# Where the second sample's half slots stand in a fused four-layer block: token layer from half slot 2, offsets projected ahead, mask summed a slot later, convolution's adds three half slots further back

## The reference, cut to what matters

```python
def reference(x, ...):                      # x: 16 x 128 x 56 x 56, f32
    x = x + _L0_conv_ref(_gn(x), ...)       # whitening of 8 channel groups
    x = x + _L1_conv_ref(_gn(x), ...)       # deformable convolution: depthwise 3x3, norm, GELU,
                                            #   offsets and mask by a matmul, mask softmax,
                                            #   bilinear samples weighted by the mask, out matmul
    x = x + _L2_conv_ref(_gn(x), ...)       # attention in 7x7 windows, a token per window,
                                            #   attention over the tokens, aggregate, out matmul
    x = x + _L3_conv_ref(_gn(x), ...)       # mask from the centre of mass, relu, 3x3 convolution
    return x
```

## Time and profile before

| | us |
|---|---|
| median of 3 runs | 11108.46 |
| lowest and highest run | 11075.77, 11125.28 |
| the profiled execution, its own time | 11137.82 |
| its span | 11135.9 |
| PE busy | 8908.2 (80% of the span) |
| DVE busy | 7395.0 (66%) |
| ACT busy | 3642.6 (33%) |
| mean granted TensorE clock | 0.848 of full speed |

### The profile page before, as it was taken

One profiled execution on the slowest core, in us unless ns is written; L12 is line 12 of the kernel. 1 busy time (PEld: TensorE's weight loads), 2 busy tenths in 40 slices (PEclk: granted clock), 3 DMA queues, 4 the chain that ended last, 5 costly groups with the idle time before them and its releaser, 6 DMA issues.

```text
span 11135.9 us, 288961 instructions
## 1 busy us (share of the span) xinstructions
PE 8908.2 (80%) x124030; PEld 4802.9 (43%) x124030; DVE 7395.0 (66%) x9080; ACT 3642.6 (33%) x5874; POOL 199.6 (2%) x254
## 2 busy tenths in 40 slices
PE   5478887887888888788888878888887888888887
PEld 5324444353443435344343534434354443435444
DVE  2476676667666776866677676667767766776663
ACT  0024333242333424233242433324243332424322
POOL 0000000000000000000000000000000000000000
PEclk7568798888978888897888989888898988889798
DMA  4001101111110111111011111101111010111101
GB/s 102 9 8 35 40 21 42 31 36 35 39 42 19 41 34 34 35 39 38 22 40 28 40 38 36 37 24 42 28 40 38 27 42 26 43 28 40 38 19 51
DMA packets 230314, 391.72 MB, mean 35 GB/s; under 512 B 25200, under 2 KB 166480, under 8 KB 221776
## 3 DMA queue, kind: packets, MB, share of 16 engines
q1 hardware_dynamic: 229008, 372.66, 12.0%
HBM read 192.47 MB, written 130.55 MB: 29 GB/s over the span
## 4 chain that ended last, share of the span: by engine, by line
PE 55%; DVE 25%; issue 12%; ACT 6%; DMA 1%; DVEq 0%; SPq 0%; POOL 0%; ACTq 0%; POOLq 0%
PE ps L875 10%; PE ps L743 7%; PE ps L678 7%; DVE arena L1679 4%; PE ps L776 4%; PE ps L751 4%; PE ps L792 3%; DVE arena L1656 3%; DVE arena L1662 3%; PE ps L974 3%; DVE arena L1739 3%; PE ps L964 3%; PE ps L765 2%; PE ps L700 2%; DVE arena L1645 1%
## 5 line engine op out<-in xcount | busy, mean ns | idle before, releaser
L875 PE MATMUL ps<-arena,ident 64*64 64x512 f32 x5600 | 2043.6, 763 | 965.9 <-DVE arena L1679 930.8
L877 PE MATMUL ps<-arena,ident 48*64 48x512 f32 x5600 | 2050.5, 764 | 0.0
L1679 DVE TENSOR_TENSOR arena<-arena 112x2560 f32<-112x2560 f32 x560 | 1573.4, 2817 | 0.5 <-PE ps L877 0.5
L875 PEld LDWEIGHTS ps<-arena,ident 64*64 64x64 f32 x5600 | 546.4, 163 | 2146.3 <-issue 2135.7
L743 PE MATMUL ps<-arena,wqk 128*128 128x400 f32 x2048 | 975.7, 602 | 175.1 <-DVE arena L1785 127.9
L1770 DVE COPY arena<-ps 128x400 f32<-128x400 f32 x512 | 293.2, 573 | 887.2 <-PE ps L743 886.0
L678 PE MATMUL ps<-vp,convw 128*128 128x448 f32 x2016 | 816.9, 550 | 23.6 <-ACT vp L1287 23.6
L1662 DVE TENSOR_TENSOR arena<-arena 112x576 f32<-112x576 f32 x1008 | 764.0, 758 | 34.9
L776 PE MATMUL ps<-ident,arena 128*128 128x128 f32 x4096 | 620.3, 300 | 206.7 <-ACT arena L1215 57.4
L792 PE MATMUL ps<-arena 64*64 64x33 f32 x32768 | 674.6, 235 | 106.9 <-issue 69.9
L751 PE MATMUL ps<-wv,arena 128*64 128x256 f32 x4096 | 657.7, 447 | 107.3 <-ACT arena L1158 95.5
(11 more groups left out here) (286 smaller groups left out, 12294.3 us busy)
## 6 DMA issues: line engine op xcount, KB each, us to landing
windows_out<-arena SPq DMA_DIRECT2D x1024, 100.0 KB
arena<-windows_out SPq DMA_DIRECT2D x224, 256.0 KB, 4.1
arena<-windows_out SPq DMA_DIRECT2D x224, 192.0 KB, 3.3
arena<-in_wqk SPq DMA_DIRECT2D x16, 2048.0 KB, 8.4
arena<-in_x_t SPq DMA_DIRECT2D x16, 1568.0 KB, 10.3
arena<-in_x SPq DMA_DIRECT2D x16, 1568.0 KB, 6.7
arena<-arena SPq DMA_DIRECT2D x32, 784.0 KB
out_x<-xb SPq DMA_DIRECT2D x112, 224.0 KB, 1.9
```

The costliest lines, as they stand in the source:

```text
L875: nc.tensor.matmul(ps[half, 3, :], ident[0:SLOT, 0:SLOT], prod[0:SLOT, ring(c, dy), dx, :], start=(s < 2), stop=(s >= TAPS - 2), skip_grou ...
L877: mm = nc.tensor.matmul(ps[half, 4, :], ident[SLOT:PT, SLOT:], prod[SLOT:PT, ring(c, dy), dx, :], start=(s < 2), stop=(s >= TAPS - 2), ski ...
L1679: V.tensor_tensor(prod[0:PT, ring(c, dy), :, :].rearrange("p k (n e) -> p k n e", e=CG), taps.to_broadcast([PT, SHIFTS, N64, CG]), for_tap ...
```

## The change

The numbers in the `if` chains become names, and the names get other values. The token layer begins at half slot 2 instead of 3; its transposes, queries and keys, scores, and everything of sample i behind them stand two half slots earlier on PE; DVE's softmax stands one earlier; relu and convolution stand two earlier (45 and from 46), so that the last row is at 66. The convolution's adds move the other way: `ADD_Q` is 52, 55, 58, 61, 64, 67, 69 where it was 51, 54, and so on to 69, while the last rows they wait for now stand at 48, 51, and so on to 66. Apart from this, PE's `project` at dy 1 goes ahead of the other sample's piece of the slot, and DVE's `sum_mask` and `norm_mask` move from the end of dy 2 to dy 3. No instruction is added or taken out.

```diff
+TOK_Q, TURN_Q, Q2_Q, S2_Q, SOFT_Q, A2_Q, AGG_Q = 2, 6, (8, 10), 12, 15, 18, 20
+GN_Q = AGG_Q + 17
+CONV_Q = [GN_Q + 9 + j for j in range(3 * CHUNKS)]
+ADD_Q = [min(at + 4, 2 * TR * SHIFTS - 7 + k) for k, at in enumerate(CONV_Q[2::3])]
...
-                elif 22 <= q < 24 + 2 * WS:
-                    if q >= 24 and q % 2 == 0:
-                        project_windows(i, (q - 24) // 2)
-                    if q < 22 + 2 * WS:
-                        aggregate(i, q - 22)
-                elif q == 39:
+                elif 0 <= q - AGG_Q < 2 + 2 * WS:
+                    h = q - AGG_Q
+                    if h >= 2 and h % 2 == 0:
+                        project_windows(i, h // 2 - 1)
+                    if h < 2 * WS:
+                        aggregate(i, h)
+                elif q == GN_Q:
                     group_mean(i, 2, 2)
-                elif 48 <= q < 48 + 3 * CHUNKS:
-                    k, dy = (q - 48) // 3, (q - 48) % 3
+                elif q in CONV_Q:
+                    k, dy = CONV_Q.index(q) // 3, CONV_Q.index(q) % 3
...
                             sum_taps(n, c, dy)
+                        if dy == 1 and c + 1 < TR:
+                            project(n, c + 1, 1)
                         if i is not None:
                             after_windows(i, 2 * s)
                         if dy == 0 and c:
                             turn_sum(n, c - 1)
                         elif dy == 1:
-                            if c + 1 < TR:
-                                project(n, c + 1, 1)
-                            else:
+                            if c + 1 == TR:
...
-                elif 51 <= q < 51 + 3 * CHUNKS and (q - 51) % 3 == 0:
-                    k = (q - 51) // 3
+                elif q in ADD_Q:
+                    k = ADD_Q.index(q)
                     dve.wait_ge(c3_p.sem, c3_p.at(i, k + 1))
...
-                        if ahead and dy == 2:
+                        if ahead and dy == 3:
                             sum_mask(n, c + 1)
                             norm_mask(n, c + 1)
-                        elif ahead and dy == 3:
                             rows_by_mask(n, c + 1)
                             by_row(n, c + 1, 0)
```

More of the change, by code:

```diff
@@ L896, in after_windows @@
             def after_windows(i, q):
-                if q == 8:
+                if q == TURN_Q:
                     pe.wait_ge(tk_g.sem, tk_g.at(i))
@@ L902, in after_windows @@
                     mm.then_inc(gt_p.sem, 1)
-                elif q in (10, 12):
-                    if q == 10:
+                elif q in Q2_Q:
+                    if q == Q2_Q[0]:
                         pe.wait_ge(gt_s.sem, gt_s.at(i))
                         pe.wait_ge(wq_in.sem, wq_in.at(i))
-                    for oc in range(2 * q - 20, 2 * q - 16):
+                    for oc in range(0, 4) if q == Q2_Q[0] else range(4, 8):
                         for kc in range(4):
@@ L910, in after_windows @@
                                                   gfT[:, kc, :], start=(kc == 0), stop=(kc == 3), skip_group_check=True)
-                    if q == 12:
+                    if q == Q2_Q[1]:
                         mm.then_inc(q2_p.sem, 1)
-                elif q == 14:
+                elif q == S2_Q:
                     pe.wait_ge(q2_s.sem, q2_s.at(i))
@@ L927, in after_windows @@
                     mm.then_inc(s2_p.sem, 1)
-                elif q == 20:
+                elif q == A2_Q:
                     pe.wait_ge(a2_s.sem, a2_s.at(i))
@@ L1251, in after_windows @@
             def after_windows(i, q):
-                if q == 4:
+                if q == TOK_Q + 1:
                     act.wait_ge(tk_v.sem, tk_v.at(i))
                     nc.scalar.activation(t8[2], t8[1], ACT.Sqrt, bias=eps_col[:, :], scale=1.0 / DH).then_inc(tk_sd.sem, 1)
-                elif q == 6:
+                elif q == TOK_Q + 3:
                     act.wait_ge(tk_s.sem, tk_s.at(i))
                     nc.scalar.activation(tok, tok, ACT.Gelu).then_inc(tk_g.sem, 1)
-                elif q == 9:
+                elif q == TURN_Q + 1:
                     act.wait_ge(gt_p.sem, gt_p.at(i))
@@ L1269, in after_windows @@
                     ins.then_inc(q2_s.sem, 1)
-                elif q == 17:
+                elif q == SOFT_Q + 1:
                     act.wait_ge(s2_m.sem, s2_m.at(i))
                     nc.scalar.activation(s2, s2, ACT.Exp, scale=SCALE).then_inc(s2_e.sem, 1)
-                elif q == 21:
+                elif q == A2_Q + 1:
                     act.wait_ge(a2_p.sem, a2_p.at(i))
@@ L1276, in after_windows @@
                                          ).then_inc(a2_t.sem, 1)
-                elif q == 40:
+                elif q == GN_Q + 1:
                     group_sqrt(i, 2)
-                elif q == 42:
+                elif q == GN_Q + 3:
                     act.wait_ge(gn_ab[2].sem, gn_ab[2].at(i))
@@ L1282, in after_windows @@
                                          ).then_inc(v3_s.sem, 1)
-                elif q == 47:
+                elif q == GN_Q + 8:
                     act.wait_ge(mk_s.sem, mk_s.at(i))
@@ L1287, in after_windows @@
                         nc.scalar.activation(vp_in[:, rows, :], mk[:, rows, :], ACT.Relu).then_inc(rl_s.sem, 1)
-                elif 23 <= q < 23 + 2 * WS and q % 2:
-                    aggregated(i, q - 23)
-                    aggregated(i, q - 22)
+                elif 0 < q - AGG_Q < 2 * WS and (q - AGG_Q) % 2:
+                    aggregated(i, q - AGG_Q - 1)
+                    aggregated(i, q - AGG_Q)
             def aggregated(i, h):
@@ L1841, in after_windows @@
             def after_windows(i, q):
-                if q == 3:
+                if q == TOK_Q:
                     owne.turn(i, DVE_END)
@@ L1872, in after_windows @@
                                     ALU.mult).then_inc(a2_s.sem, 1)
-                elif 26 <= q < 26 + 2 * WS and q % 2 == 0:
-                    nb = (q - 26) // 2
+                elif 0 <= q - AGG_Q - 4 < 2 * WS and (q - AGG_Q) % 2 == 0:
+                    nb = (q - AGG_Q - 4) // 2
                     dve.wait_ge(y2_p.sem, y2_p.at(i, nb + 1))
@@ L1883, in after_windows @@
                         group_stats(owne, i, 2)
-                elif q == 40:
+                elif q == GN_Q + 1:
                     group_variance(owne, i, 2, 2)
-                elif q == 41:
+                elif q == GN_Q + 2:
                     group_scale(owne, i, 2)
-                elif q == 43:
+                elif q == GN_Q + 4:
                     dve.wait_ge(v3_s.sem, v3_s.at(i))
                     owne.mark(V.tensor_reduce(rsum[:, 0:W], vp_in, AX.X, ALU.add))
-                elif q == 44:
+                elif q == GN_Q + 5:
                     owne.step(V.tensor_tensor(mk[:, 0:28], vp_in[:, 0:28], vp_in[:, 28:56], ALU.add))
```

12 lines of the change are left out of this document (6 added, 6 removed).

## The result

| | before | after |
|---|---|---|
| median, us | 11116.87 (4 runs) | 10797.77 (4 runs) |
| lowest and highest run | 11075.77, 11132.11 | 10794.42, 10818.51 |
| span of the profiled execution | 11135.9 | 10792.5 |
| mean granted clock | 0.848 | 0.865 |

What follows compares the result with a forecast made beforehand. Neither engine was full over a tile stage; the lead was taken to alternate between PE and DVE. Terms 5.7 + 0.4 + 16.0 = 22.1 us per sample, times 15 is 332, off 11108 gives 10776 us; range 10620 to 10980.

Steps and rivals of the forecast that it cites:

- The early term: Slots 2 to 9, token layer and projection: shorter DVE waits for projection and exponential, gain 5.7 us per sample.
- the small end: Slots 2 to 9: gain 0 if slot 4's taps and queries run wholly at half clock.
- The middle term: Slots 10 to 18, the aggregate: slot 24 starts 0.4 us earlier per sample, net of DVE's owed work.
- PE 8.5 earlier: Aggregate: PE's last window projection ends 8.5 us earlier, with 5.8 and 11.2 as ends.
- The large end of 11.2: Aggregate: the most by which PE's last window projection was to end earlier, 11.2 us.
- The last term: Slots 23 to 34, convolution and adds: PE gaps and slow taps go, 16.0 us per sample, bounds 10 and 19.
- rival (a): Only the adds count; early gain eaten by slow taps, new rows stay slow: 10.2 per sample, 10955 us, chance 0.15.
- My own sentence on gaps: PE's taps run at half clock behind gaps of 4 to 14 us, mostly at full behind shorter ones.
- (b): From slot 24, DVE's list sets the end, not PE: 25 more gained per sample, 10400 us, chance 0.04.
- (c): Waits only move: DVE waits for taps instead of at adds, PE's gaps stay: 11100 us, chance 0.06.
- (d): Slots 12 to 18: DVE and PE in lock-step at the window projection, 255 us slower, 11365 us, chance 0.07.
- The promised signs: Changed profile: tile stage 335 us, convolution wait near 50, projection waits a third to half lower, slot 29's gap gone.

Runs made afterwards that it cites:

- both kernels with the tokens' loads first: Changed kernel with two token loads issued ahead of the 2 MB load: ratio 0.9708; the same with the projection back behind the other sample's piece: 0.9663.
- the shift alone: Changed kernel with mask and projection moves undone and each add one half slot behind its chunk's last row; other sample's pieces stay earlier: ratio 0.9994.
- less PE work: Changed kernel without the last convolution tap in each of the seven chunks, 7 matmuls fewer per sample: 10730.57 us, ratio 0.9717.
- more DVE work: Changed kernel with one more DVE pass over the mask (mask + mask, never read) in slot 28: 10784.58 us, ratio 0.9761.

## Why the prediction was right, and where it was off

**The early term, 5.7: right in size on the average (4.9), by luck in part.** Slots 4 to 9 fell from 47.7 to 42.7 us, and in sample 1 DVE's wait for slot 6's projection is the 4.6 where I had worked out 4.3:

```profile
1231.11 0.46 DVE L1628 TENSOR_REDUCE softmax_max<-ps 112x32 f32<-112x288 f32 x1 [4.60 <-PE ps L705]
```

That is so in 7 of the 15 bodies only (4.0 to 5.1 us). In the other 8, sample 2 among them, it is 7.92:

```profile
1876.82 0.46 DVE L1628 TENSOR_REDUCE softmax_max<-ps 112x32 f32<-112x288 f32 x1 [7.92 <-PE ps L705]
```

PE's timeline shows why: the first half of the queries, in slot 4, runs at the full clock in one and at the lower level in the other (slot 4's taps before it ended at full clock in the first, and were slow to the last in the second).

```profile
1213.81 3.79 PE L914 MATMUL ps<-arena 128*128 128x64 f32 x32
...
1854.29 7.09 PE L914 MATMUL ps<-arena 128*128 128x64 f32 x32
```

The 7 bodies take 39.6 us from slot 4 to slot 9, the 8 take 45.4. Before there were two kinds as well, by the same 3.8 or 7.1 us of that half, which then stood in slot 5: 10 bodies of 45.1 us and 5 of 52.8. I had worked from the ten. Against them the seven gained 5.5 us, as forecast, and the eight nothing, which is the small end that I had named ("if slot 4's taps and queries run wholly at the half clock") and had given no weight in the sum. The five bodies with waits near 16 us, which my sum left out, made the average good.

I also gave 1.55 of the term to the mask, and had the projection ahead of the other piece as part of it. The runs show that the queries' earlier place does it: the shift alone won 8.3 and putting the projection back lost nothing (42.3). The 3.3 us that the mask's move costs here are the eight bodies of the slow kind: with the mask put back, and in the shift alone, all 30 bodies have these queries at full clock, as have both kernels with the tokens' loads first. How many bodies are slow changes from kernel to kernel even where the orders up to slot 9 are the same (8 in the changed kernel, 7 with less PE work, 2 with more DVE work), and with it the average by 2 us. What decides it was not tested.

**The middle term, 0.4: a small gain forecast, a small loss measured.** Slots 12 to 24 took 145.4 us instead of 144.3. My step "PE 8.5 earlier" was too large: counted from slot 9's product, the last window projection ended 4.8 us earlier in sample 1 and 6.1 on the average. The stall of 1.95 us ahead of slot 15's taps, which I let go, is still there (1.92, with slow taps behind it), and a wait of 2 us of the aggregate for ACT was new. The large end of 11.2 was also mis-added: the pieces named for it (4.0, 1.3, 1.95, 2.6) come to 9.9. The other half held: DVE owed its list, and PE stands 9.07, 3.77, 3.95, 4.83 and 2.12 us for products between slots 19 and 23. Busy time from 1354 to the first row of the convolution shows which engine is full there:

```profile
1354.00:1408.20 54.20, 30.45 (x131) 10.64 (x129) 52.59 (x55) 17.13 (x28) 1.43 (x1) 0.69 0.00 1
```

DVE is busy 52.59 of 54.20 us. So this kernel changes its bound twice in a tile stage, as the prediction said: DVE here, PE from slot 24 on.

**The last term, 16.0: 14.3 measured.** From slot 24's product to the copy it went from 112.4 to 98.0 us. Up to slot 34's taps the sum was even low: 98.8 to 81.1, 17.7 us. The missing part is in the tail, which I had not looked at: from the start of slot 34's taps to the copy it takes 13.3 us on the average instead of 10.6 (13.6 in sample 1), at a lower clock (below). Its parts: the adds alone gave 9.3 from slot 24 to the copy, and the shift on top of them 5.0. The part of rival (a) by which the new rows stay slow is out: in sample 1 they took 2.52 and 2.42 us, the same as any other row, although the stretch up to them ran at 0.69; over the 15 bodies the first took 2.52 to 3.07 us and the second always 2.42. The Trainium skill, TensorE: Matmul & The Clock Gate, What's actually happening, says the slow clock is the default and activity releases it; slot 23's taps (0.61 us for the first record, 4.5 us for all twenty instead of 2.8) were still partly slow, the row right behind them was not. So the trace agrees, only the clock rose one piece sooner than the rival needed. My own sentence on gaps does not hold as it stands: behind gaps of 4 us and more no taps of the 15 bodies before ran wholly at full clock, but behind those of 1 to 4 us only 33 of 132 did, and the earlier trace rows has slow taps behind 2.66.

**The rivals.** (a) Only the adds count: 10.0 of the 17.9 us per tile stage are theirs, and in 8 of 15 bodies the early gain was eaten by a slow clock, much as this rival says; but the shift behind them gave 9.0 more. (b) DVE's list is ruled out by the two runs on PE's and DVE's work. (c) Waits only move: true of the projection alone and of the shift alone, false of the adds. (d) The lock-step did not come: slots 12 to 18 took 1.3 us less, though DVE's wait for the window projection grew from 278.4 to 571.9; PE, busy 50.48 us of the 54 from 1300 to 1354, paid nothing.

**The promised signs.** The tile stage fell by 17.9 us to 340.5, where 357 to 335 promised 22. PE's 7.59 gap gone, no slow taps behind slot 25, PE 100% busy: as promised. The projection's wait fell by 25%, not by a third or more. The wait for the convolution is 152, not 50: I missed that the last add, capped at half slot 69, waits 7.05 us for the last row now that DVE is ahead. PE's wait for the product fell by 162 us, just past the 150 below which I would have called myself wrong: it counts gaps at products, not the slow taps behind them. And the 14 us gap before slot 23's taps, which was to stay, did not: it is 1.6 to 4.2 us, while a new one of 9.06 stands ahead of slot 19's taps in all 15 bodies, where there was none, and others of up to 5 us between them.

**Parts that made up for each other.** Of 332 us forecast the tile stages gave 268, and 75 came from the three terms that I had set at nothing. One of these is real: 16 us in the first tile stage come from the mask's move in every run that has it (257 to 262 us, against 278 in those that have it not). I had put that stage at nothing because no other sample runs in it, though the mask's wait for the exponential is there too. The 57 us of the windows stages are mostly not the change's: in the other runs, with the same code there, they took 293.0 to 296.5 us on the average, whether the change was in or not. So the forecast time was closer than its terms deserve: they were 64 us too large where I counted, and luck in the windows stages gave 57 back.

## What to carry to other kernels

Where two engines feed each other through a ring of two, cost a consumer's wait by what is queued behind it: an add that stands one half slot behind its producer held DVE 9.4 us and then PE 7.6, and three half slots more were worth 10 us a sample. An earlier start of the producer is worth nothing (here 0.9994) or less (1.0045) as long as the consumer moves up with it, and 9 us once it stays behind, so try the parts together and take each out again, rather than only one at a time. Look at every body of the loop before taking a wait from one: here two neighbouring samples differ by 6 us in the same five slots. And look at what a load stands behind in its queue: two loads of 64 KB behind one of 2 MB landed after 7.4 us instead of 2.2.

## What the runs showed of the hardware

**The clock falls behind a full stretch too.** Busy time by stretch around the end of slot 34's taps, after:

```profile
1491.50:1500.70 9.20, 9.20 (x47) 2.79 (x46) 0.68 (x1) 0.00 (x0) 0.00 (x0) 1.00 0.09 31
1500.70:1510.50 9.80, 7.11 (x23) 4.28 (x23) 1.41 (x4) 2.26 (x4) 0.51 (x4) 0.64 0.01 3
```

The same place before:

```profile
1542.50:1551.30 8.80, 8.80 (x37) 3.56 (x35) 1.09 (x2) 0.00 (x0) 0.00 (x0) 1.00 0.08 31
1551.30:1559.10 7.80, 5.09 (x26) 3.21 (x24) 1.39 (x4) 2.26 (x4) 0.49 (x4) 1.00 0.02 4
```

Both come out of back-to-back work at 1.00, and both meet the same wait of 1.3 us for ACT. Before, the turn and the out projection ran at full clock; after, the clock fell to its lower level (1.2 GHz) during the turn, and the granted clock is 0.64 over the stretch. PE's timeline has the out projection's first half there, with

```profile
1505.10 1.86 PE L898 MATMUL ps<-xa,ident 128*128 128x448 f32 x2 [0.63 <-ACT arena L1248]
```

instead of 1.02 us for its two records. The same 1.86 stands there in 11 of the 15 loop bodies and 1.24 to 1.72 in the other four; before, it is 1.02 in all 15. It goes with the 2.7 us that the average body loses from slot 34's taps to the copy. Why the one falls and the other not, with PE busier beforehand in the one that falls, no run here settles.

**The same work at two clocks.** Two windows stages of the kernel after, by stretch, the sixth and the second of the loop:

```profile
4062.22:4347.46 285.24, 235.67 (x4866) 148.03 (x4864) 195.62 (x280) 137.06 (x211) 3.42 (x7) 0.91 0.14 36
1510.55:1811.32 300.77, 252.24 (x4867) 156.20 (x4865) 196.00 (x281) 137.24 (x211) 3.44 (x7) 0.86 0.13 34
```

The matmuls are the same to one, the DVE and ACT times too; the granted clock differs, and 15.5 us with it.

**The first tile stage: half a wait, half a clock.** It got shorter with not one instruction less. Before:

```profile
623.15:901.49 278.34, 223.42 (x931) 82.22 (x932) 217.68 (x173) 58.55 (x112) 7.71 (x10) 0.69 0.02 6
```

After:

```profile
621.11:883.23 262.12, 186.31 (x931) 71.05 (x932) 217.25 (x173) 58.13 (x112) 7.71 (x10) 0.80 0.02 7
```

PE is busy 37 us less for the same 931 matmuls. DVE is busy as long as before, so what it waits for tells where the 16 us went. Its waits in these two windows, before:

```profile
DVE softmax_max L1622 <- PE ps L700: 32.0, 6, 5.8
...
DVE softmax_sum L1632 <- ACT arena L1227: 8.3, 6, 1.6
DVE near L1687 <- PE ps L994: 4.4, 1, 4.4
```

After:

```profile
DVE softmax_max L1628 <- PE ps L705: 28.7, 6, 7.7
...
DVE near L1693 <- PE ps L1000: 0.4, 1, 0.4
```

The wait for the exponential, 8.3 us, is gone: the mask's later place covers it, as I had said of the loop, and it is a wait for ACT, not for PE. Another 7.3 us are shorter waits for PE, whose granted clock in this stage is 0.80 instead of 0.69. With the mask's move alone the three waits are 25.0 us, none and 0.4; with the mask put back they are 31.9, 8.3 and 4.3. That the later place changed the spacing of PE's pieces, and so their clock, is likely but was not tested by itself.
